# A convolution group of 8 channels ahead of the first gate product, and the second tile's down product inside its own step

## What is computed

```python
def reference(u, D, Lambda_re, Lambda_im, log_dt, W_re, W_im, w_gate, w_up, w_down):
    x = u
    xn = _layernorm(x, axis=-1)
    # attn: k from the complex exponentials, 128 taps; causal convolution; + xn * D
    s = _L0_attn_ref(xn, D, Lambda_re, Lambda_im, log_dt, W_re, W_im)
    # ffn: q() rounds blocks of 16 to the FP4 grid
    #   h = silu(q(xn) @ q(w_gate).T) * (q(xn) @ q(w_up).T);  g = silu(q(h) @ q(w_down).T)
    g = _silu(_L0_ffn_ref(xn, w_gate, w_up, w_down))
    return x + s * g
```

## Time and profile before

| | |
|---|---|
| three runs | 666.48, 666.35, 663.82 us; median 666.35 us |
| the profiled execution | 663.84 us, of which the span of the profile is 662.0 us |
| PE busy | 496.4 us (75%) |
| DVE busy | 586.4 us (89%) |
| ACT busy | 403.7 us (61%) |
| convolution steps, 260 to 510 us of the span | PE busy 243.30 of 250 us, DVE 223.12, ACT 158.65 |
| granted TensorE clock in those steps | 1.00 |

### The profile page before, as it was taken

How to read it: one execution, slowest core, us unless ns; L and a number is a source line. 1 busy time by engine, 2 the same in 40 slices (tenths; PEclk the granted TensorE clock), 3 DMA queues, 4 the chain that set the end, 5 groups by cost and what they waited for, 6 DMA issues and landing times.

```text
span 662.0 us, 13047 instructions
## 1 busy us (share of the span) xinstructions
PE 496.4 (75%) x4856; PEld 342.4 (52%) x4856; DVE 586.4 (89%) x690; ACT 403.7 (61%) x562; POOL 214.2 (32%) x301
## 2 busy tenths in 40 slices
PE   0000067757788888999999999999999848798895
PEld 0000045323555555777677777767676525455564
DVE  7999999799789989899988899998989858879887
ACT  7960187764878876666666666666666545453654
POOL 1229620044444444111111123231121373747320
PEclk9999996798789989999999999999999989979999
DMA  6950000101000013555555555555552199935324
GB/s 199 348 162 0 0 0 16 33 1 27 14 17 17 16 49 95 158 149 144 145 144 147 151 162 156 162 144 149 154 149 84 22 200 209 181 90 117 75 64 128
DMA packets 109218, 70.80 MB, mean 107 GB/s; under 512 B 9072, under 2 KB 108912, under 8 KB 109168
## 3 DMA queue, kind: packets, MB, share of 16 engines
q1 hardware_dynamic: 101776, 62.73, 32.5%
q0 software_dynamic: 7392, 7.34, 7.6%
HBM read 61.28 MB, written 8.78 MB: 106 GB/s over the span
## 4 chain that ended last, share of the span: by engine, by line
PE 34%; DVE 31%; DMA 15%; issue 9%; POOL 5%; ACT 3%; SPq 2%; ACTq 0%; DVEq 0%; POOLq 0%
PE ps L1203 12%; DMA work<-kpad 12%; PE ps L1221 8%; PE ps L1223 4%; DVE work L849 3%; DVE wgu L936 3%; PE ps L1236 3%; DMA gbuf<-L_attn_u 3%; PE ps L1240 3%; DVE work L844 3%; PE ps L1212 3%; DVE sm L791 2%; DVE work L883 2%; SPq L393 1%; DVE work L875 1%
## 5 line engine op out<-in xcount | busy, mean ns | idle before, releaser
L1203 PE MATMUL ps<-wgu,work 128*128 128x512 f16 (+1 forms) x1152 | 242.9, 366 | 7.8 <-DVE work L875 6.6
L1203 PEld LDWEIGHTS ps<-wgu,work 128*128 128x128 f16 x1152 | 112.3, 99 | 116.6 <-issue 8.6
L614 ACT ACTIVATE work<-ps,con 128x704 f32<-128x704 f32 x64 | 54.2, 848 | 110.7 <-PE ps L1203 110.7
L609 ACT COPY work<-ps 128x1408 f16<-128x1408 f16 x64 | 84.8, 1324 | 18.4 <-PE ps L1212 18.2
L1221 PE MATMUL ps<-wdh,work 128*128 128x256 f16 x704 | 93.2, 284 | 2.7 <-ACT work L609 2.0
L844 DVE SCALAR_TENSOR_TENSOR work<-work 128x960 f32<-128x960 bf16 (+2 forms) x67 | 80.9, 1218 | 13.6 <-ACT work L629 13.5
L1212 PE MATMUL ps<-id,work 128*128 128x128 f16 x704 | 51.6, 224 | 52.0 <-DVE work L883 22.0
L875 DVE TENSOR_TENSOR work<-work,ps 128x704 f32<-128x704 f32 x64 | 56.5, 883 | 34.1 <-ACT work L614 34.0
L510 POOL TENSOR_TENSOR gbuf<-gbuf,xh 128x512 f32<-128x512 f32 x28 | 40.6, 1476 | 111.6 <-DVE work L857 96.1
L1221 PEld LDWEIGHTS ps<-wdh,work 128*128 128x128 f16 x704 | 69.1, 102 | 12.2 <-ACT work L609 2.2
L1212 PEld LDWEIGHTS ps<-id,work 128*128 128x128 f16 x704 | 41.8, 100 | 61.9 <-issue 32.1
(11 more groups left out here) (151 smaller groups left out, 766.2 us busy)
## 6 DMA issues: line engine op xcount, KB each, us to landing
work<-kpad SPq DMA_DIRECT2D x64, 512.0 KB, 4.8
gbuf<-u_rev SPq DMA_DIRECT2D x4, 2048.0 KB, 18.4
work<-L_attn_u SPq DMA_DIRECT2D x32, 256.0 KB, 4.6
gbuf<-L_attn_u POOLq DMA_DIRECT2D x14, 512.0 KB, 6.3
out<-gbuf SPq DMA_DIRECT2D x14, 512.0 KB, 4.2
work<-L_attn_u SPq DMA_DIRECT2D x2, 512.0 KB, 4.2
work<-L_ffn_w_down SPq DMA_DIRECT2D x1, 704.0 KB, 6.6
work<-L_ffn_w_gate SPq DMA_DIRECT2D x1, 640.0 KB, 4.5
```

The lines of the kernel that those rows point to most:

```text
L609: nc.scalar.copy(hT[par], src).then_inc(hT_a, 1)
L1203: last = T.matmul(p_gu[:, a:b], xT[par][:, t, c, :], wgu[:, part, c % 2, a:b], start=(n == 0), stop=(n == len(todo) - 1))
```

## The change

In the convolution steps PE multiplies group A right after the first `h_transpose`, ahead of the first `gate_up`, where before it stood behind the first tile's `down`. The `down` of the second tile, which stood behind the first `h_transpose` of the following step, now ends its own step, behind group B. ACT's `y_copy` of group A moves with it: ahead of the first `silu_gate` instead of behind the first `silu_out`. Step 8 itself still begins with the `down` left over from step 7. The instructions and their number are the same on every engine, and the code of SP, DVE and POOL is not touched.

```diff
@@ ACT, step
                 if a2:
                     a_scale(it * 2)
+                if cv:
+                    y_copy(it * 2 - 2 * S_CONV)
                 if gu:
                     silu_gate(it * 2)
                 square(it, 1 - par, x, ch, 0)
@@
                     silu_out(it * 2 - 4, 0, par)
-                if cv:
-                    y_copy(it * 2 - 2 * S_CONV)
                 if td:
                     h_copy(it * 2 - 3, 1)
@@ PE, step
             def step(it, par, x, gu, td, cv=False):
+                c8 = (it - S_CONV) * 2
                 if td:
                     pe.wait_ge(hl_v, it - 1)
                     h_transpose(it * 2 - 4, 0, par)
-                    if it > 2:
+                    if it > 2 and not S_CONV < it <= S_OUT:
                         down(it * 2 - 5, 1)
+                if cv:
+                    pe.wait_ge(a_lp, NT // 4)
+                    conv(c8, 0)
+                    conv(c8, 1)
                 if gu:
                     gate_up(it * 2, 0, par, it + 1)
                 if x:
                     x_transpose(it + 1, 1 - par)
                 if td:
                     down(it * 2 - 4, 0)
-                if cv:
-                    pe.wait_ge(a_lp, NT // 4)
-                    conv(it * 2 - 2 * S_CONV, 0)
-                    conv(it * 2 - 2 * S_CONV, 1)
-                if td:
                     h_transpose(it * 2 - 3, 1, par, copied=it + 2 if x else None)
                 if gu:
                     gate_up(it * 2 + 1, 1, par, None)
                 if cv:
-                    conv(it * 2 - 2 * S_CONV + 1, 0)
-                    conv(it * 2 - 2 * S_CONV + 1, 1)
+                    conv(c8 + 1, 0)
+                    conv(c8 + 1, 1)
+                    down(it * 2 - 3, 1)
```

## The result

The changed kernel takes 730.01 us (median of four runs, 726.57 to 732.12), the kernel before 666.41 us. The ratio is 1.096, 95% interval 1.091 to 1.101: **9.6% slower**. The profiled execution took 730.9 us with a span of 729.1 us.

What follows compares the result with a forecast made beforehand. PE's own chain of work was taken to bound the convolution steps, losing 0.62 us per step to band loads. The sum 663.84 + 42 + 5.9 + 1.9 + 12 = 725.6 was given as 725 us, range 701 to 744 us.

Steps and rivals of the forecast that it cites:

- (1): Convolution steps, between A1 and B1: 10.8 us of work cover the band loads, so today's 0.62 us per step goes.
- (2): From B1's end to the next A1, 15 seams: 3.19 us of work against a 6.1 us turnaround, 2.9 us stall.
- the slope that I drew from the loads of the kernel before: Fourth band load, behind B: landing 5.6 us at about 1 us spacing, 4.8 at 1.5, so about 5.9 at 0.72.
- both of my values: Turnaround from B1's end to A1: 6.1 us taken, 5.35 us if the x load does not slow its neighbour.
- (3): Second h transposing of each convolution step: PE waits for ACT's copy of the x transposing, +0.52 us.
- (4): Convolution steps: ACT's 0.7 us copy of group A hidden by gate product, moved down product finds its operand ready: nothing.
- (5): Step 8, once: PE idles for POOL's last low part with 5.87 us of work still to do, +5.9 us.
- (6): Low clock behind idle waits of PE: +1.9 us in step 8, +12 us at 7 of 15 seams, 1.66 us each.

Runs made afterwards that it cites:

- the four buffers: Changed kernel with four band buffers instead of two, each load issued two halves earlier: 672.50 us, ratio 1.007.
- the x load run: Changed kernel, but SP issues the 256 KB x load between the loads behind A and those behind B: 721.30 us, ratio 1.086.
- step 8 run: Changed kernel with group A and ACT's copy of it back behind the first down product in step 8 only: 717.33 us, ratio 1.080.
- The filled kernel: Changed kernel with unused products in each seam's idle stretches, nine ahead of A0 and seven ahead of A1: 714.38 us, ratio 1.069.
- the balanced order: Kernel before, two buffers, group A moved ahead of the first tile's down product, behind the x transposing: 657.13 us, ratio 0.984.
- either filled kernel: The filled kernel, 714.38 us, and the kernel before with group A's move alone plus five and seven unused products, 712.78 us.

## Why the prediction was right, and where its sizes were off

725 us were forecast, 730 measured; the mechanism and its place were right. That the number came so near is in part luck: the turnaround was forecast too long, the low clock too seldom, and how often the clock falls differs from run to run of one kernel. Step by step:

- **Loads for B hidden (1).** Right: no wait ahead of B in the trace.
- **The seam's stall (2).** Taken at a turnaround of 6.1 us, it was 5.87, so 2.7 us instead of 2.9. That it is the reload and not the order itself is shown by the four buffers (672.5 us). The reasoning for 6.1 was wrong: the second load of a seam landed after 5.40 us on the mean, not 5.9, so the slope that I drew from the loads of the kernel before did not go on to a spacing of 0.7 to 0.8 us; and moving the x load out of the way took off 0.16 us where I had reckoned with 0.5 or more. To both of my values 0.2 us were added from the chain's end of B1, 0.16 us later than the start of the next instruction, from which the 5.87 and the 3.19 us of work count; that made up for a part. Between A and B the second load landed after 5.14 us before, in the seams of the x load run after 5.26; differences so small, with single loads from 4.6 to 6.5 us, are not settled.
- **ACT's copy (3).** 0.52 us from the waits of PE; from start to start the same place costs 0.68 us, for the end of the row before is modelled 0.16 us late. The two errors in (2) and (3) cancel: per step 15.39 + 0.68 + 2.68 = 18.75 us without the clock, 18.8 forecast, so 41 us instead of 42.
- **No cost for ACT's copy of A and for the late down product (4).** Right: 665.4 us with the down product moved alone, and with four buffers, where the copy stands in its new place too, a period of 16.06 us that leaves nothing for either.
- **Step 8 (5).** The wait for POOL ended at 259.42 as forecast, with 5.87 us of work still to do. It is 5.07 us long and not 6.8, because the down product ahead of it ran at the low clock in this execution (with four buffers, where it did not, the wait is 6.71). A and the gate product behind it took 7.16 us instead of 5.00, the 2.2 us counted below, forecast as 1.9:

```profile
250.04 1.03 PE L1212 MATMUL ps<-id,work 128*128 128x128 f16 x11 [2.17 <-DVE work L883]
250.87 2.55 PE L1221 MATMUL ps<-wdh,work 128*128 128x256 f16 x11
253.22 1.13 PE L1223 MATMUL ps<-wdl,work 128*128 128x256 f16 x6
...
259.42 0.34 PE L1236 MATMUL ps<-xh,work 128*128 128x64 f16 x3 [5.07 <-POOL xh L500]
...
261.97 4.77 PE L1203 MATMUL ps<-wgu,work 128*128 128x512 f16 x18
266.58 0.61 PE L1191 MATMUL ps<-id,work 128*128 128x128 f16 x8
```

The run that undoes it shows 8.5 us between the traces, in line with 5.9 + 2.2; its median is too widely scattered to confirm the size.
- **The clock (6).** The term that was mis-sized. I took 7 of 15 seams at 1.66 us, 12 us, and no row gave that count; it was 12 of 15, at 1.6 us each (A1 and the gate product behind it), 19 us. The step 8 run, with the same seams, had 8. The filled kernel shows the term: with the clock at 1.00 it is 15.6 us faster, although its turnaround is 0.28 us longer, which costs 4 us. The Trainium skill, page "TensorE: Matmul & The Clock Gate", section "HAM oscillation — how this bites in real kernels", describes the low clock in every round. The trace of the changed kernel has it in 12 of 15 rounds, nearer to that than my 7, the trace of the step 8 run in 8.

Sum of the measured terms: 663.84 + 41 + 5.9 + 2.2 + 19 = 732 us, against the profiled execution's 730.9.

## What to carry to other kernels

For work that reloads its own buffers in a cycle, write down the work between freeing a buffer and needing it again, for each point of the cycle: it is the smallest of these covers that stalls, not their sum. Here the covers were 4.9 and 9.1 us before, 10.8 and 3.2 after, and 6.8 and 7.2 in the balanced order, against a turnaround of 5 to 7 us; only the last has no stall. And price an idle TensorE twice, for the wait itself and for the products behind it at the low clock: in this trace 41 us and 19 us.

## What the runs showed of the hardware that was not expected

Where the same instructions are idle for the same time, the clock falls in one step and not in the next. In the steps ahead of the convolution, which every kernel here runs alike, PE waits for DVE's rounded h. The twelve traces have 33 such waits of 2.13 to 2.22 us between 150 and 258 us. After 16 of them a stretch at 1.2 GHz followed, after 17 none. Step 8 shows it in one place: after a wait of 2.17 us the changed kernel's transposing took 1.03 us, and that of the same kernel with four buffers 0.79. So the length of a wait does not tell by itself what follows; what does is open, and a single case, such as the wait of 2.18 us in the filled kernel that was followed by no low clock, proves little. What the runs do show is the count: 12, 8 and 8 low seams of 15 (the changed kernel, the step 8 run, the x load run) with the idle time in two pieces and 24 short matrix instructions between them, 5 of 15 with somewhat less idle time in three pieces and a down product between, none of 15 in either filled kernel.

The turnaround is uneven, 5.3 to 6.9 us. In the trace of the changed kernel five of the 15 seams had no instruction fetch on queue q8 among the transfers between the end of B1 and A1 (one of the five had a small one on queue q14); their turnaround was 5.3 to 6.0 us, mean 5.5. The ten with one on queue q8 had 5.4 to 6.9, mean 6.0. In the x load run it is five with 5.0 to 5.8, mean 5.3, and ten with 5.1 to 6.9, mean 5.9. The queues in such a slow stretch, 294.52 to 301.97 us (packets, MB, share of 16 engines):

```profile
q1 hardware_dynamic: 2348, 1.31, 59.5%
q8 instruction: 1, 0.02, 1.1%
```

The fetch moves hardly any bytes, so if it is the cause, then not by its bandwidth. This was seen and not tested.
